# Projections as three float16 products of parts, and a later rope sum, in a macaron layer kernel

## The reference

```
x = x + 0.5 * ffn(layernorm(x), w_gate_up, w_proj)
x = x + attention(layernorm(x), Wq, bq, Wk, bk, Wv, bv, Wo, bo)
x = x + 0.5 * ffn(layernorm(x), w_gate_up, w_proj)
```

## Time and profile before

| | us |
|---|---|
| median of 3 runs | 3103.22 |
| the profiled execution, own time | 3101.82 |
| its span | 3100.0 |
| first ffn layer, from the start to | 780.9 |
| projections, first to last add_bias | 793.2 to 990.0 |
| attention, from | 1004.5 |

### The profile page before, as it was taken

One profiled execution on the slowest core, in us unless ns is written; L12 is line 12 of the kernel. 1 busy time (PEld: TensorE's weight loads), 2 busy tenths in 40 slices (PEclk: granted clock), 3 DMA queues, 4 the chain that ended last, 5 costly groups with the idle time before them and its releaser, 6 DMA issues. The chain is left out here.

```text
span 3100.0 us, 61305 instructions
## 1 busy us (share of the span) xinstructions
PE 2967.1 (96%) x20310; PEld 1183.7 (38%) x20310; DVE 1867.4 (60%) x2221; ACT 1739.7 (56%) x3220; POOL 795.3 (26%) x772
## 2 busy tenths in 40 slices
PE   7889999999998999999999999999997999999999
PEld 4434444444564122222222222222233444444444
DVE  6852222221676999999999999999723222222221
ACT  5643333333111499999999999999910333333332
POOL 0144444444443000000000000000022444444444
PEclk9999999999999799999999999999989999999999
DMA  4311110011333011111111111111356011111100
GB/s 130 110 52 41 41 39 16 27 41 42 91 104 104 10 33 31 31 31 31 31 31 30 30 30 31 31 30 30 101 166 226 13 41 41 41 41 41 41 14 28
DMA packets 163904, 160.58 MB, mean 52 GB/s; under 512 B 62552, under 2 KB 100824, under 8 KB 163808
## 3 DMA queue, kind: packets, MB, share of 16 engines
q1 hardware_dynamic: 163808, 159.30, 17.8%
HBM read 111.48 MB, written 47.19 MB: 51 GB/s over the span
## 5 line engine op out<-in xcount | busy, mean ns | idle before, releaser
L1780 DVE TENSOR_REDUCE at_neg_max<-at_max_ps 128x1 f32<-128x1024 f32 x1024 | 1174.4, 1217 | 39.7 <-PE at_max_ps L1636 38.8
L1763 ACT ACTIVATE at_probs<-at_score_ps 128x512 f32<-128x512 f32 x2048 | 1116.7, 597 | 75.4 <-PE at_score_ps L1656 46.4
L1636 PE MATMUL at_max_ps<-at_km,at_q 48*128 48x512 f16 x2048 | 634.7, 390 | 19.1 <-DVE at_neg_max L1780 8.8
L1656 PE MATMUL at_score_ps<-at_q,at_ks 50*128 50x512 f16 x2048 | 627.5, 384 | 24.5 <-DMA at_q<-at_max_parts 19.5
L1665 PE MATMUL at_out_ps<-at_probs,at_v 128*32 128x256 f32 x8192 | 644.7, 393 | 3.4
L983 DVE SCALAR_TENSOR_TENSOR f_h<-f_up_ps,hr_factor,f_gate 128x512 f32<-128x512 f32 x128 | 96.1, 751 | 475.3 <-ACT f_gate L1057 473.2
L1725 POOL CAST at_max_parts<-at_max_rows 16x128 f16<-16x128 f32 x64 | 17.9, 280 | 1182.8 <-ACT at_max_rows L1736 1182.8
L413 DVE SCALAR_TENSOR_TENSOR f_h<-f_up_ps,hr_factor,f_gate 128x512 f32<-128x512 f32 x112 | 83.9, 749 | 393.4 <-PE f_up_ps L752 240.0
L1665 PEld LDWEIGHTS at_out_ps<-at_probs,at_v 128*32 128x32 f32 x8192 | 169.1, 109 | 394.8 <-issue 211.7
L1656 PEld LDWEIGHTS at_score_ps<-at_q,at_ks 50*128 50x128 f16 x2048 | 132.2, 94 | 448.1 <-ACT at_probs L1763 396.1
L1057 ACT ACTIVATE f_gate<-f_gate_ps 128x512 f32<-128x512 f32 x128 | 76.4, 597 | 353.0 <-PE f_up_ps L1130 353.0
(11 more groups left out here) (149 smaller groups left out, 3738.3 us busy)
## 6 DMA issues: line engine op xcount, KB each, us to landing
rows<-x SPq DMA_DIRECT2D x40, 1024.0 KB, 5.6
x<-rows SPq DMA_DIRECT2D x16, 1024.0 KB, 4.6
f_raw<-units SPq DMA_DIRECT2D x48, 256.0 KB, 2.7
at_q<-qk_parts SPq DMA_DIRECT2D x384, 32.0 KB, 1.8
rows<-x SPq DMA_DIRECT2D x32, 256.0 KB, 2.8
at_q<-at_max_parts SPq DMA_DIRECT2D x512, 1.0 KB
att<-at_out SPq DMA_DIRECT2D x256, 32.0 KB
out<-rows SPq DMA_DIRECT2D x8, 1024.0 KB, 4.2
```

The lines of the kernel that those rows point to most:

```text
L1636: done = nc.tensor.matmul(max_ps[u % 2][:, half * QB:(half + 1) * QB], q[k][rows, j // SLOTS, h * QB + c * P:h * QB + (c + 1) * P], km[k][ ...
L1656: nc.tensor.matmul(score_ps[pos % RING][:], ks[k][rows, kc * P:(kc + 1) * P], q[k][rows, j // SLOTS, h * QB:(h + 1) * QB], start=True, sto ...
L1763: nc.scalar.activation(probs[:, kc % PBUF, j, :], score_ps[pos % RING][:], ACT.Exp, scale=HD ** -0.5).then_inc(exps, 1)
L1780: nc.vector.tensor_reduce(neg_max[:, h, column:column + 1], max_ps[u % 2][:], AX.X, ALU.max, negate=True).then_inc(maxed, 1)
```

## The change

`product` no longer multiplies float32 by float32. ScalarE's copy of the turned rows now writes float16 (`xt_hi`), VectorE writes the remainder (`xt_lo`, new stage `low_turned`), the weights are split once at the start of the block (`w_hi` on ScalarE, `w_lo` on VectorE), scaled by powers of two that `Balance` computes, and the product is the sum of hi*hi, hi*lo and lo*hi. `add_bias` undoes the scale, in two pieces. `Balance` measures the value part too and has seven more tiny instructions (`take_ranges`, chunk 9). In VectorE's order `rotate` has lag 4 in place of 3 and stands ahead of `add_bias`; `low_turned` (lag 2) opens the step.

```diff
     def measure_rest(self, dve):
-        w, b = self.parts[1]
-        dve.tensor_reduce(self.largest[:, 1:2], w, ...)
-        for k in range(2):
-            dve.tensor_reduce(self.largest[:, 2 + k:3 + k], self.parts[k][1], ...)
+        for k in (1, 2):
+            dve.tensor_reduce(self.largest[:, k:k + 1], self.parts[k][0], ...)
+        for k in range(3):
+            dve.tensor_reduce(self.largest[:, 3 + k:4 + k], self.parts[k][1], ...)
...
+    def take_ranges(self, dve):
+        dve.tensor_tensor(self.top[:, 0:1], self.exponent[:, 1:2], self.exponent[:, 0:1], ALU.subtract)
+        dve.tensor_scalar(self.top[:, 1:2], self.exponent[:, 2:3], 0.0, None, ALU.add)
+        dve.tensor_scalar(self.held[:], self.top[:], 20.0, 250.0, ALU.max, ALU.min)
+        dve.tensor_scalar(self.raise_by[:], self.held[:], -1.0, 2.0 * 127 + 14, ALU.mult, ALU.add)
+        dve.tensor_scalar(self.lower_by[:], self.held[:], 14.0, None, ALU.subtract)
+        dve.tensor_scalar(self.raising_bits[:], self.raise_by[:], 23, None, ALU.logical_shift_left)
+        dve.tensor_scalar(self.lowering_bits[:], self.lower_by[:], 23, None, ALU.logical_shift_left)
...
                 dve.wait_ge(prods, i + 1)
-                nc.vector.tensor_tensor(rows[:, k, :], row_ps[k][:, 0:FALL], bias, ALU.add).then_inc(biased, 1)
+                for n, (c0, c1) in enumerate(((0, FA), (FA, FALL))):
+                    last = nc.vector.scalar_tensor_tensor(
+                        out=rows[:, k, c0:c1], in0=row_ps[k][:, c0:c1], scalar=balance.lowering[:, n:n + 1],
+                        in1=bias[:, c0:c1], op0=ALU.mult, op1=ALU.add)
+                last.then_inc(biased, 1)
+
+            def low_weights(n, c0, c1):
+                dve.wait_ge(w_high, n + 1)
+                nc.vector.scalar_tensor_tensor(
+                    out=w_lo[:, :, c0:c1], in0=w_qkv[:, :, c0:c1], scalar=balance.raising[:, n:n + 1],
+                    in1=w_hi[:, :, c0:c1], op0=ALU.mult, op1=ALU.subtract).then_inc(w_low, 1)
+
+            def low_turned(i, k):
+                k %= 2
+                dve.wait_ge(turned_high, i + 1)
+                nc.vector.tensor_tensor(xt_lo[:, k], turn_ps[k][:], xt_hi[:, k], ALU.subtract).then_inc(copied, 1)
+                if isinstance(i, int) and i == 0:
+                    low_weights(0, 0, FA)
+                    low_weights(1, FA, FALL)
...
-            steps(nc, dve, NSUB, [(0, row_stats), (0, stats_made), (5, low_part), (0, row_moments),
-                              (1, normalise), (3, add_bias), (3, cosine), (3, rotate)], unroll=RX, peel=RX)
+            steps(nc, dve, NSUB, [(2, low_turned), (0, row_stats), (0, stats_made), (5, low_part), (0, row_moments),
+                              (1, normalise), (4, rotate), (3, add_bias), (3, cosine)], unroll=RX, peel=RX)
...
-                nc.scalar.copy(xt[:, k % 2], turn_ps[k % 2][:]).then_inc(copied, 1)
+                nc.scalar.copy(xt_hi[:, k % 2], turn_ps[k % 2][:]).then_inc(turned_high, 1)
...
+            for n, (c0, c1) in enumerate(((0, FA), (FA, FALL))):
+                nc.scalar.activation(w_hi[:, :, c0:c1], w_qkv[:, :, c0:c1], ACT.Copy,
+                                     scale=balance.raising[:, n:n + 1]).then_inc(w_high, 1)
...
+                if isinstance(i, int) and i == 0:
+                    pe.wait_ge(w_low, 2)
                 for c0, c1 in ((0, FQ), (FQ, FALL)):
                     for c in range(DC):
-                        last = nc.tensor.matmul(row_ps[k][:, c0:c1], xt[:, k, c, :], w_qkv[:, c, c0:c1],
-                                                start=(c == 0), stop=(c == DC - 1))
+                        for x_part, w_part in ((xt_hi, w_hi), (xt_hi, w_lo), (xt_lo, w_hi)):
+                            last = nc.tensor.matmul(row_ps[k][:, c0:c1], x_part[:, k, c, :], w_part[:, c, c0:c1],
+                                                    start=(c == 0 and w_part is w_hi and x_part is xt_hi),
+                                                    stop=(c == DC - 1 and x_part is xt_lo))
```

More of the change, by code:

```diff
@@ L92, in sem @@
             return ctx.enter_context(nc.semaphore(f"bl_{n}"))
-        self.parts = [(w_qkv[:, :, 0:FQ], bias[:, 0:FQ]), (w_qkv[:, :, FQ:FA], bias[:, FQ:FA])]
+        self.parts = [(w_qkv[:, :, c0:c1], bias[:, c0:c1]) for c0, c1 in ((0, FQ), (FQ, FA), (FA, FALL))]
         self.w_in, self.ones = w_in, ones
[L96 to L99, removed]
+        self.largest = sb("largest", [P, 6], F32)
+        self.total = sb("total", [P, 6], F32)
+        self.size = sb("size", [P, 3], F32)
+        self.exponent = sb("exponent", [P, 3], mybir.dt.int32)
+        self.top = sb("top", [P, 2], mybir.dt.int32)
+        self.held = sb("held", [P, 2], mybir.dt.int32)
+        self.raise_by = sb("raise_by", [P, 2], mybir.dt.int32)
+        self.lower_by = sb("lower_by", [P, 2], mybir.dt.int32)
+        self.raising_bits = sb("raising", [P, 2], mybir.dt.int32)
+        self.lowering_bits = sb("lowering", [P, 2], mybir.dt.int32)
+        self.raising, self.lowering = self.raising_bits[:].bitcast(F32), self.lowering_bits[:].bitcast(F32)
         self.half = sb("half", [P, 1], mybir.dt.int32)
@@ L113, in measure_rest @@
     def measure_rest(self, dve):
-        w, b = self.parts[1]
-        dve.tensor_reduce(self.largest[:, 1:2], w, AX.XY, ALU.max, apply_absolute_value=True).then_inc(self.measured, 1)
-        for k in range(2):
-            dve.tensor_reduce(self.largest[:, 2 + k:3 + k], self.parts[k][1], AX.X, ALU.max,
+        for k in (1, 2):
+            dve.tensor_reduce(self.largest[:, k:k + 1], self.parts[k][0], AX.XY, ALU.max,
+                              apply_absolute_value=True).then_inc(self.measured, 1)
+        for k in range(3):
+            dve.tensor_reduce(self.largest[:, 3 + k:4 + k], self.parts[k][1], AX.X, ALU.max,
                               apply_absolute_value=True).then_inc(self.measured, 1)
     def total_over_rows(self, pe, ps):
-        pe.wait_ge(self.measured, 4)
-        pe.matmul(ps[:, 0:4], self.ones, self.largest[:], start=True, stop=True).then_inc(self.summed, 1)
+        pe.wait_ge(self.measured, 6)
+        pe.matmul(ps[:, 0:6], self.ones, self.largest[:], start=True, stop=True).then_inc(self.summed, 1)
     def take_factors(self, dve, ps):
         dve.wait_ge(self.summed, 1)
-        dve.tensor_copy(self.total[:], ps[:, 0:4]).then_inc(self.copied, 1)
+        dve.tensor_copy(self.total[:], ps[:, 0:6]).then_inc(self.copied, 1)
         dve.wait_ge(self.copied, 1)
-        dve.tensor_tensor(self.size[:], self.total[:, 0:2], self.total[:, 2:4], ALU.add).then_inc(self.sizing, 1)
+        dve.tensor_tensor(self.size[:], self.total[:, 0:3], self.total[:, 3:6], ALU.add).then_inc(self.sizing, 1)
         dve.wait_ge(self.sizing, 1)
@@ L142, in take_factors @@
         dve.tensor_scalar(self.factor[:], self.biased[:], 23, None, ALU.logical_shift_left).then_inc(self.sizing, 1)
+    def take_ranges(self, dve):
+        dve.tensor_tensor(self.top[:, 0:1], self.exponent[:, 1:2], self.exponent[:, 0:1],
+                          ALU.subtract).then_inc(self.sizing, 1)
+        dve.tensor_scalar(self.top[:, 1:2], self.exponent[:, 2:3], 0.0, None, ALU.add).then_inc(self.sizing, 1)
+        dve.wait_ge(self.sizing, 9)
+        dve.tensor_scalar(self.held[:], self.top[:], 20.0, 250.0, ALU.max, ALU.min).then_inc(self.sizing, 1)
+        dve.wait_ge(self.sizing, 10)
+        dve.tensor_scalar(self.raise_by[:], self.held[:], -1.0, 2.0 * 127 + 14, ALU.mult,
+                          ALU.add).then_inc(self.sizing, 1)
+        dve.tensor_scalar(self.lower_by[:], self.held[:], 14.0, None, ALU.subtract).then_inc(self.sizing, 1)
+        dve.wait_ge(self.sizing, 12)
+        dve.tensor_scalar(self.raising_bits[:], self.raise_by[:], 23, None, ALU.logical_shift_left).then_inc(self.sizing, 1)
+        dve.tensor_scalar(self.lowering_bits[:], self.lower_by[:], 23, None, ALU.logical_shift_left).then_inc(self.sizing, 1)
     def apply(self, dve, k):
@@ L488, in tile @@
                             balance.take_factors(dve, size_ps)
+                        if c == 9:
+                            balance.take_ranges(dve)
                         if c == HC - 2:
@@ L1216, in projection_loads, with projections @@
     return rope, x_in, load
-def projections(nc, x, rope, x_in, load, w_qkv, bias, w_in, qk_parts, v_rows, ident, neg_half,
+def projections(nc, x, rope, x_in, load, w_qkv, balance, bias, w_in, qk_parts, v_rows, ident, neg_half,
                 before, n_starts, start_next, v_out, parts_out):
@@ L1240, in projections @@
         rstd = sb("rstd", [P, 2], F32)
-        xt = sb("xt", [P, 2, DC, P], F32)
+        xt_hi = sb("xt_hi", [P, 2, DC, P], F16)
+        xt_lo = sb("xt_lo", [P, 2, DC, P], F16)
         rows = sb("rows", [P, 2, FALL], F32)
@@ L1246, in projections @@
         low = sb("low", [P, 2, NF, 2 * P], F16)
+        w_hi = sb("w_hi", [P, DC, FALL], F16)
+        w_lo = sb("w_lo", [P, DC, FALL], F16)
```

(5 more changed lines are left out.)

## The result

The changed kernel takes 3078.91 us (median of 4 runs, 3072.70 to 3079.92) against 3101.24 for the kernel before (4 runs, 3099.01 to 3103.26): a ratio of 0.9925, 95% interval 0.9911 to 0.9939. The forecast was 3094.4, the range 3082 to 3107. The profiled execution took 3079.74 us (span 3077.9), 22.1 less than that of before.

The account below looks back on a forecast made before the run. Two limits bound a step: the sine chain (6.37 us) and TensorE (6.24). With a 6.03 loop and start +4.8, add_bias(31) came 9.0 sooner; less 0.2, 3093.0 profiled, 3094.4 median; range 3082 to 3107.

Parts of the forecast that it names:

- What rotate runs into: VectorE's rotate waits for GpSimd's root and ends at 1.15 us in place of 0.82: +0.33, loop 6.03.
- first rival: Rotate is not held up by root: loop 5.70 us, 8.9 us less, 3085.5; chance 0.22.
- 2.09 from the end of rotate to low_turned: Chain rotate, features, turn, ScalarE's copy, low_turned takes 2.09 us; low_turned waits 0.25; loop 5.70 with rotate free.
- two limits lay close together: Before the change, the chain through the sine at 6.37 us a step and TensorE at 6.24, 0.13 apart.
- The product, 3.9 us: TensorE's float16 product takes 3.9 us a step (bounds 3.8 and 5.2), 256-column matmuls at 0.11 each.
- low_turned's 0.60 and add_bias's 1.17: VectorE per step: 0.60 us added by low_turned; two-piece add_bias takes 1.17 until cosine, against 0.98.
- ScalarE's split free, the start +4.8: ScalarE's weight split costs nothing; VectorE's split and the half clock put the first add_bias at 798.0, +4.8 us.
- No wait of add_bias for the product: In full steps the product ends 5.4 us after rotate's end and is not late for add_bias.
- the tail: Behind the last add_bias, SyncE's queue and the last low_part move along unchanged: 0 us.
- the first layer: Added reductions and seven tiny instructions mostly fit VectorE's idle time: 0.2 us with rounding, up to 2 uncovered.
- The rivals of the other side: Saving lost to slow 256-column matmuls (3101 to 3105), chance 0.16; slower by clock or held low_turned, together 0.10.
- The prediction's clock rival: TensorE falls to 1.2 GHz in the loop, 10.0 us work a step, some 3220; chance 0.10 with held low_turned.

Follow-up runs that it names:

- order_only: The kernel before with only VectorE's order changed (rotate at lag 4 ahead of add_bias), float32 product kept: ratio 0.9983, step 6.15 us.
- wide_before_root: The changed kernel with one more GpSimd product of 320 columns ahead of root: 3096.93 us in a single run, step 6.05 us.
- product_only: The changed kernel with rotate back at lag 3, behind cosine at the end of the step: ratio 1.0071, step 7.16 us.
- small_before_root: The changed kernel with two more one-column GpSimd products ahead of root: 3078.86 us in a single run, step 5.53 us.
- low_turned_in_gap: The changed kernel with rotate back at lag 3 and low_turned between cosine and rotate: ratio 1.0061, step 6.86 us.

## Why the prediction was wrong

**The failed step** is "What rotate runs into": +0.33 for rotate behind root. Measured +0 (0.82 in all 28 steps of the change in which root runs beside it, and 0.82 in order_only). The formula for a held instruction was right (wide_before_root, to 0.02 us); what failed is that root is such a case. The prediction carried it over from L661, a GpSimd product of 512 columns on the page of the first layer, to an operation of one column, and named this as the doubt in its first rival. That rival, chance 0.22, was the true case. Over 27 steps the term is 27 x 0.33 = 8.9 us, of the 13.3 by which the profiled execution was missed (3093.0 against 3079.7).

**The second term, mis-sized:** 2.09 from the end of rotate to low_turned. Measured (918.37 to 920.28) 1.91: features start 0.06 after rotate, not 0.15; features to turn 0.60, not 0.63; turn to the copy 0.63, not 0.70. All three were taken from the loop of before; why they are shorter here was not tested. For the first, the row itself has a hint: at 811.07, where its features start, TensorE had only just left its product (805.83 + 5.16 = 810.99), so up to 0.07 of the 0.15 may not be the distance from VectorE. With 1.91 the chain and VectorE's own 1.83 meet, low_turned waits 0.08 rather than 0.25, and the free loop is 5.53, not 5.70: 27 x 0.17 = 4.6 us. So even the rival's 3085.5 was too high, and the range, which ended 3.5 us below it, missed by 3.1. The two terms, 13.5 together, explain the loop to 0.1 us: 5.56 x 27 = 150.2 from add_bias(1) to add_bias(28) against 163.6, 13.4 less. The ends nearly cancel: first interval 4.72 for 4.35, the last three 5.37, 4.89, 4.44 for 5.4, 5.0, 4.55.

**Right:** that two limits lay close together (0.23 apart, by order_only) and either edit alone would be stopped by the other (order_only at TensorE, product_only at the sine). The prediction didn't say that the product alone would lose 22 us, though its own numbers (low_turned 0.60, add_bias +0.19 on the sine's chain) give it. The product, 3.9 us with 256 columns at 0.109. low_turned's 0.60 and add_bias's 1.17. ScalarE's split free, the start +4.8 against 4.82, half clock included. No wait of add_bias for the product in full steps.

**Smaller:** the tail is 0.67 longer, counted at nothing; and the first layer, charged with 0.2, was 1.4 shorter; order_only, whose first layer is that of before, came to the stage 2.7 us sooner than before, so 1.4 is within what two executions differ by.

**The rivals of the other side** did not come: the clock was 1.00 from 800 to 960 us (last section), low_turned was not stretched under the sine (0.69), and the 256-column matmuls took half the time of the 512-column ones.

## What to carry to other kernels

When two limits are within a few per cent, work out each edit alone and both together from the chains, with each new instruction put on its chain: here one alone gave 0.2%, the other alone lost 0.7%, both gave 0.75%. When a price hangs on contention, match the row it is taken from in what it streams, not only in engine and operands; if no row of that size exists, let both cases carry weight and let the range reach past the better one. Three distances between engines, taken over from another loop, were 0.03 to 0.09 too long each: times the number of steps, such a small error belongs in the range. And a test of contention must be read one instruction at a time: a merged row of two small operations showed an engine busy that was in fact being held.

## What the hardware showed unexpectedly

**GpSimd and VectorE.** An operation of 320 columns held a two-SBUF-input VectorE instruction until it was over (0.82 to 1.34 us); root, of one column, begun 0.29 us ahead (922.79, rotate at 923.08), did not. The other way round rotate held one-column operations: in small_before_root one of 0.19 us took 0.66 and ended 0.05 behind rotate, and behind the wide operation, root of 0.77 us took 1.12, over the stretch in which the held rotate got its columns (893.60 to 894.72). The Trainium skill (SBUF — State Buffer, Who interferes with whom) has the pair of ports locked by whoever issues first for the whole instruction. The 320-column case agrees, and so do the operations that rotate held. Root does not: by that rule rotate would have started its columns at root's end (923.56) and ended at 924.23, and the trace has 923.90. The measurement decides. A reading that would fit all of them, not tested: root reads its column early and holds nothing afterwards. Root takes 0.55 us at the start of the stage (781.55), 0.77 when it begins beside normalise and then ends 0.40 after normalise (923.56, 923.16), and in wide_before_root it ends 0.40 after rotate (894.72, 894.32). So of its 0.77 us the first part would be a wait, and its read would be over before rotate's columns begin (923.90 - 0.67 = 923.23).

**The clock.** The stretch from 800 to 960 us in the change, in low_turned_in_gap and in product_only, in this order (columns as in the earlier trace rows):

```profile
800.00:960.00 160.00, 147.26 (x953) 94.53 (x952) 155.41 (x285) 34.21 (x58) 87.92 (x87) 1.00 0.39 112
```

```profile
800.00:960.00 160.00, 116.95 (x764) 75.74 (x763) 128.64 (x234) 28.32 (x48) 72.32 (x71) 1.00 0.33 95
```

```profile
800.00:960.00 160.00, 124.91 (x730) 75.84 (x731) 121.23 (x226) 25.96 (x44) 67.49 (x67) 0.94 0.31 89
```

TensorE kept the full 2.4 GHz in the first two and lost it in part of the third (0.94). In product_only some steps have matmuls of 512 columns at 0.43 us apiece, 1.2 GHz, and TensorE pauses 1.96 us a step for low_part, against 1.72 in low_turned_in_gap. The busy times do not rank the two: at 1.2 GHz a matmul is shown for longer, and in the stretches of product_only at full clock TensorE is busy 14.66 of 20 us (860 to 880) and 14.11 (920 to 940), about the 14.6 of 20 of low_turned_in_gap. What decides is not shown by these runs. The prediction's clock rival, which product_only comes nearest to, was real though not for the change. Its step was not made longer by it, as 6.38 + 0.79 gives its length without the clock. The Trainium skill (TensorE: Matmul & The Clock Gate, Part 4: PE-mode transpose) says that transposes do not count as activity in the way matmuls do; in the change, with 3.9 of 5.53 us in the product, the clock held, which neither bears that out nor speaks against it.
